# The MLP pairs of a four-layer vision transformer: transpositions moved into the second product, normalised rows first on VectorE

## What is computed

```python
for i in range(DEPTH):                         # DEPTH = 4
    ...                                        # attention: h = h + proj(attn(layernorm(h)))
    y = layernorm(h, ln2_w[i], ln2_b[i])
    y = gelu(y @ fc1_w[i] + fc1_b[i])          # 128 -> 256
    h = h + (y @ fc2_w[i] + fc2_b[i])          # 256 -> 128
```

## Time and profile before

| | |
|---|---|
| median of 3 runs | 4076.8 us (4069.07 to 4085.77) |
| the profiled execution: its time, its span | 4077.07 us, 4075.3 us |
| mean granted clock of PE | 0.945 of full speed |
| PE busy | 3523.8 us, 86% of the span |
| DVE, POOL, ACT busy | 2503.2, 2284.3, 1907.3 us |
| PE in 500 to 600 us (attention) | 96.54 us busy, 1129 matmuls |
| PE in 1400 to 1500 us (MLP of layer 1) | 85.25 us busy, 602 matmuls |
| PE in 2700 to 2800 us (mostly MLP of layer 3) | 85.41 us busy, 641 matmuls |

### The profile page before, as it was taken

The page is one execution under the profiler, slowest core; times in us unless marked ns, Lnnn a source line. Parts: engine busy times, 40 slices in busy tenths (PEclk is TensorE's granted clock), DMA queues, the critical chain, the costliest instruction groups (busy, mean ns, idle before and its releaser), DMA issues. The chain is left out here.

```text
span 4075.3 us, 91248 instructions
## 1 busy us (share of the span) xinstructions
PE 3523.8 (86%) x30780; PEld 2731.6 (67%) x30780; DVE 2503.2 (61%) x6419; ACT 1907.3 (47%) x3468; POOL 2284.3 (56%) x2633
## 2 busy tenths in 40 slices
PE   8779999888999888999987999988698887876983
PEld 8747777657777666777765777766344665655763
DVE  1246776546677555777654677755796887975110
ACT  0036666435666633666643666653464443322421
POOL 0056665465566366666446666625695663264876
PEclk9969999989999998999999999999898998998987
DMA  6556666025666314666502666620110223132432
GB/s 222 173 97 122 124 126 114 8 55 98 119 129 124 66 19 79 122 127 127 110 8 55 115 127 125 125 38 1 43 33 21 59 63 52 27 100 45 70 59 29
DMA packets 456050, 341.98 MB, mean 84 GB/s; under 512 B 70659, under 2 KB 440171, under 8 KB 455595
## 3 DMA queue, kind: packets, MB, share of 16 engines
q1 hardware_dynamic: 413635, 314.62, 37.5%
q0 software_dynamic: 27136, 16.42, 3.0%
q10 hardware_dynamic: 15008, 7.51, 0.7%
HBM read 227.69 MB, written 109.29 MB: 83 GB/s over the span
## 5 line engine op out<-in xcount | busy, mean ns | idle before, releaser
L720 DVE TENSOR_REDUCE a_neg_max<-a_S 99x4 f32<-99x788 f32 x1024 | 1003.5, 980 | 566.8 <-PE a_S L351 552.7
L533 ACT ACTIVATE a_probs<-a_St 99x792 f32<-99x792 f32 (+1 forms) x1024 | 851.2, 831 | 683.8 <-PE a_St L368 672.5
L368 PE MATMUL a_St<-a_q_st,a_k_st 99*99 99x198 bf16 (+1 forms) x4096 | 529.7, 252 | 90.5 <-DMA a_q_st<-a_max_rows 75.8
L351 PE MATMUL a_S<-a_k_st,a_q_st 96*99 96x197 bf16 x4096 | 552.1, 258 | 44.4 <-DVE a_neg_max L720 44.2
L351 PEld LDWEIGHTS a_S<-a_k_st,a_q_st 96*99 96x99 bf16 x4096 | 399.7, 128 | 266.5 <-DVE a_neg_max L720 220.4
L368 PEld LDWEIGHTS a_St<-a_q_st,a_k_st 99*99 99x99 bf16 (+1 forms) x4096 | 391.2, 126 | 122.5 <-DMA a_q_st<-a_max_rows 69.1
L385 PE MATMUL a_O<-a_probs,a_v_aug 99*32 99x198 f32 (+1 forms) x8192 | 466.4, 340 | 0.3
L663 POOL TENSOR_TENSOR h<-h,a_rows 99x512 f32<-99x512 f32 x128 | 162.8, 1272 | 275.1 <-DVE a_m_xn L801 275.1
L385 PEld LDWEIGHTS a_O<-a_probs,a_v_aug 99*32 99x32 f32 (+1 forms) x8192 | 247.0, 110 | 84.8 <-issue 2.1
L631 POOL CAST a_max_parts<-a_neg_max 99x32 bf16<-99x32 f32 x128 | 27.1, 212 | 471.1 <-DVE a_neg_max L720 471.1
L512 PEld LDWEIGHTS a_O<-a_w,a_gelu 128*99 128x99 f32 x2048 | 239.9, 167 | 45.0 <-issue 28.6
(11 more groups left out here) (263 smaller groups left out, 7314.2 us busy)
## 6 DMA issues: line engine op xcount, KB each, us to landing
xpatch<-in_x SPq DMA_DIRECT2D x64, 594.0 KB, 3.7
spill_q<-a_parts SPq DMA_DIRECT2D x384, 99.0 KB
spill_k<-a_parts SPq DMA_DIRECT2D x384, 99.0 KB
a_k_st<-spill_k SPq DMA_DIRECT2D x128, 297.0 KB, 4.2
a_q_st<-spill_q SPq DMA_DIRECT2D x128, 297.0 KB, 6.4
a_k_st<-spill_k SPq DMA_DIRECT2D x128, 198.0 KB, 4.7
a_q_st<-spill_q SPq DMA_DIRECT2D x128, 198.0 KB, 6.7
a_k_st<-spill_k SPq DMA_DIRECT2D x128, 99.0 KB, 5.0
```

What stands on the lines that cost most here:

```text
L351: mm = nc.tensor.matmul(S[0:TC, j // 2, j % 2 * TB:j % 2 * TB + NTOK], q_st[p % 4][0:SPLIT, head, b * TB + c * TC:b * TB + (c + 1) * TC], ...
L368: mm = nc.tensor.matmul(St[0:keys, j // 2, j % 2 * TB:(j % 2 + 1) * TB], k_st[p][:, head, first:first + keys], q_st[p][:, head, b * TB:(b ...
L533: nc.scalar.activation(probs[0:keys, u % 4, :].rearrange("p (x t) -> p x t", x=2), St[0:keys, :, 0:2 * TB], ACT.Exp).then_inc(s["probs"], 1)
L720: nc.vector.tensor_reduce(out.rearrange("p (x y) -> p x y", x=2), S[0:TC, :, 0:2 * TB].rearrange("p x (y t) -> p x y t", y=2)[:, :, :, 0:N ...
```

## The change

On PE, a helper `down(t)` issues the matmuls of one tile of L512. A call of `mlp` now issues L502 of pair k + 1, tile 0 of pair k, the waits and the four transpositions of pair k + 2, then tiles 1 to 3 of pair k, the last of which signals `m_fc2`. On DVE, L801 of pair k + 2 goes ahead of L795 and L809 of pair k + 3. The order on POOL and ACT isn't touched.

```diff
--- before.py
+++ after.py
@@ -492,6 +492,13 @@
 
                 def mlp(l, k, done):
                     m = layer_w[l]
+
+                    def down(t):
+                        for h in range(2):
+                            mm = nc.tensor.matmul(O[0:TC, t * D:(t + 1) * D], gl[k % 2][:, h, t * TC:(t + 1) * TC],
+                                                  m.w2[:, h * D:(h + 1) * D], start=(h == 0), stop=(h == 1))
+                        return mm
+
                     if 0 <= k + 1 < PAIRS:
                         n = at(l, k + 1)
                         if k == -1:
@@ -507,20 +514,20 @@
                             wait(pe, s["o_copied"], 2 * at(l, PAIRS))
                         wait(pe, s["m_gelu"], 2 * (n + 1))
                         wait(pe, s["m_h"], n)
-                        for t in range(4):
-                            for h in range(2):
-                                mm = nc.tensor.matmul(O[0:TC, t * D:(t + 1) * D], gl[n % 2][:, h, t * TC:(t + 1) * TC],
-                                                      m.w2[:, h * D:(h + 1) * D], start=(h == 0), stop=(h == 1))
-                        mm.then_inc(s["m_fc2"], 1)
+                        down(0)
                     if 0 <= k + 2 < PAIRS:
-                        n = at(l, k + 2)
-                        wait(pe, s["m_xn"], n + 1)
-                        wait(pe, s["m_yT"], n)
+                        n2 = at(l, k + 2)
+                        wait(pe, s["m_xn"], n2 + 1)
+                        wait(pe, s["m_yT"], n2)
                         wait(pe, s["yT"], at(l + 1, done + 6))
                         wait(pe, s["max_copied"], at(l + 1, done + 2))
                         for t in range(4):
-                            mm = nc.tensor.transpose(M2[:, t * TC:(t + 1) * TC], m_xn[n % 2][:, t, :], g.ident[0:TC, 0:TC])
+                            mm = nc.tensor.transpose(M2[:, t * TC:(t + 1) * TC], m_xn[n2 % 2][:, t, :], g.ident[0:TC, 0:TC])
                         mm.then_inc(s["m_turned"], 1)
+                    if 0 <= k < PAIRS:
+                        for t in range(1, 3):
+                            down(t)
+                        down(3).then_inc(s["m_fc2"], 1)
 
                 program(prep, attn, mlp)(pe)
 
@@ -786,6 +793,12 @@
                         row_max(l, i + 2, p + 2, 4)
 
                 def mlp(l, k, done):
+                    if 0 <= k + 2 < PAIRS:
+                        n = at(l, k + 2)
+                        wait(dve, s["m_rstd"], n + 1)
+                        wait(dve, s["m_turned"], n - 1)
+                        nc.vector.tensor_tensor(m_xn[n % 2][:], g.h[0:TC, (k + 2) * 4:(k + 3) * 4, :],
+                                                m_rstd[n % 2][:].to_broadcast([TC, 4, D]), ALU.mult).then_inc(s["m_xn"], 1)
                     if 0 <= k + 3 < PAIRS:
                         n = at(l, k + 3)
                         q = n % 2
@@ -794,12 +807,6 @@
                         for t in range(4):
                             op = nc.vector.bn_stats(m_stats[q][:, t, :], g.h[0:TC, (k + 3) * 4 + t, :])
                         op.then_inc(s["m_stats"], 1)
-                    if 0 <= k + 2 < PAIRS:
-                        n = at(l, k + 2)
-                        wait(dve, s["m_rstd"], n + 1)
-                        wait(dve, s["m_turned"], n - 1)
-                        nc.vector.tensor_tensor(m_xn[n % 2][:], g.h[0:TC, (k + 2) * 4:(k + 3) * 4, :],
-                                                m_rstd[n % 2][:].to_broadcast([TC, 4, D]), ALU.mult).then_inc(s["m_xn"], 1)
                     if 0 <= k + 3 < PAIRS:
                         n = at(l, k + 3)
                         q = n % 2
```

## The result

The changed kernel takes 4027.43 us (median of four runs, 4020.78 to 4032.26) where the kernel before took 4076.88 beside it (four runs, 4069.07 to 4085.77): a ratio of 0.9885, with 95% between 0.986 and 0.991. The forecast was 4016, its range 4001 to 4038. The profiled execution took 4020.78, 56.3 less than that of before.

What follows compares the result with a forecast made beforehand. PE, idle in each MLP pair for ACT's copy, was taken to bound the kernel. Gains of 3 x 13.3 + 24.0 = 63.9 us, less 2.4 for overlap, made 61.5: 4077.07 to 4016 us, range 4001 to 4038.

Steps and rivals of the forecast that it cites:

- Ordinary pair: MLP pair without preparation or attention steps: 4.28 us falls to 3.48, gaining 0.80, with ACT's copy covered by matmuls.
- POOL's ring: Loop through POOL and DVE from one xn (L801) to the next: 3.31 us, under PE's 3.48 by 0.17.
- Rivals 1, 3 and 4: In ordinary pairs: POOL loop at 3.8 us, 4043, chance 0.11; gain only 0.15, 4072, 0.04; slower, 4108, 0.03.
- rival 4: PE waits for late xn ahead of twelve matmuls that h needs: pair 4.54 us, total 4108, chance 0.03.
- Layer 3: Last layer's MLP stage, without attention blocks or preparation: 30 intervals at 0.80, a gain of 24.0 us.
- Preparation and pair 9: Layers 0 to 2: weight preparation on PE comes whole, 2.35 us, -2.0 a layer; xn late behind pair 9, -1.0.
- +0.38 for two intervals: Behind pairs 13 and 25, layers 0 to 2, where PE waits for POOL's xn: 0.38 us gained over two intervals.
- +0.38 for three: Behind pairs 17 and 21, layers 0 to 2, where POOL first makes bf16 parts: 0.38 us gained over three intervals.
- nothing gained: Behind pair 29, layers 0 to 2, scores and row maxima alternate between PE and DVE: no gain up to E(30).
- Rival 2: Longer PE standstill ahead of L451 brings the 1.2 GHz clock in 15 blocks: 16 us back, 4032, chance 0.07.
- A denser PE speaks against it: Argument against the clock falling to 1.2 GHz behind the longer standstill at L451; that case had chance 0.07.
- The overlap: In attention blocks, DVE's xn (L801) and POOL's L624 meet: 0.2 us each, 12 times, 2.4 us, from 0 to 8.

Runs made afterwards that it cites:

- e1: Changed kernel's PE order with DVE's order as in the kernel before (stats ahead of xn): 4101.37 us, ratio 1.0015 to the kernel before.
- e5: Changed kernel with DVE's old order behind pairs 13 to 29 and twelve unread matmuls in PE's standstill there, layers 0 to 2: 3998.64 us, ratio 0.98.
- e3: Changed kernel, but behind pairs 13, 17, 21, 25 and 29 DVE does xn after stats, so POOL's L631 runs first: 4032.75 us, ratio 0.9835.
- e4: Changed kernel with eight unread matmuls on PE behind pairs 13 to 29 in layers 0 to 2: 4019.63 us, ratio 0.98.
- e11: Kernel before, old orders, with eight unread matmuls behind pairs 13 to 25 and three behind scores: 4074.95 us, ratio 0.9958.
- e9: Changed kernel with DVE's old order in blocks, POOL's attention deviation earlier, two tiles ahead of the transpositions, and unread matmuls behind pairs and scores: 4005.87 us, ratio 0.9782.
- e2: Kernel before with only DVE's order changed, xn ahead of stats: 4087.52 us, ratio 0.9972 to the kernel before.

## Why the prediction was right, and where not

The side and the range were right, and so was the mechanism; 4016 was 11 us low by the medians, 5 us by the profiled executions (56.3 of 61.5). That it came so near is in part luck: layers 0 and 1 gained 8.2 and 3.5 us more than layer 2, because before had lost more there to its clock, and no term of the forecast had that. By its own steps:

- **Ordinary pair.** Forecast 3.48, measured 3.42. The four transpositions take their slot of 0.34 (2074.67 - 2074.32 = 0.35), not 0.40. 0.06 x 87 = 5 us more gain. No wait is left on PE; xn's slack and POOL's ring (3.31, measured 3.33) hold as worked out. Rivals 1, 3 and 4 did not come. e1 is rival 4's loop with its condition made true: 4.02.
- **Layer 3.** Forecast 24.0, measured 25.95: 24.75 from 29 ordinary intervals and 1.20 from the one without transpositions (4.28 to 3.08).
- **Preparation and pair 9.** Forecast 2.35 over the ordinary pair, measured 16.20 - 4 x 3.42 = 2.52, 0.17 more. Pair 9: forecast 1.0, measured 4.42 - 3.42 = 1.00.
- **The blocks: the step that failed.** "+0.38 for two intervals", "+0.38 for three" and "nothing gained" behind 29. In layer 2, with the ordinary intervals that belong to each, E(12) to E(14) is 11.56 + 3.42 = 14.98 (forecast 11.92); block 17 12.84 + 6.84 = 19.68 (18.80); 21 15.09 + 6.84 = 21.93 (18.81); 25 17.39 + 3.42 = 20.81 (22.20); 29 19.62 (17.28). Together 8.0 us lost. 13.3 + 0.4 (the first transpositions, which lie ahead of the first h) + 1.1 for 19 ordinary pairs - 0.2 - 8.0 = 6.6; measured 6.5. The sums for 13, 17 and 21 were right for a clock that stays (e5: 11.88, 18.80, 18.80). What the forecast put at nothing there was the clock behind a longer standstill. The 22.20 for 25 was taken from rows of before at the low clock; e5 has 18.05.
- **What took its place.** Rival 2, which the forecast priced as if it came wholly or not at all: 16 us at 0.07. It came in part. The standstill was worked out as 2.9 and is 2.95 without the collision (e3), 3.45 with it. Behind 13 the clock now fell in every layer, where before it had fallen in two of three; over the twelve blocks 13 to 25 the first product took more than 1.49 in nine before and in twelve after. It fell at different points: behind 13 at the end of the standstill, behind 17 and 25 only among the products that follow L451 (0.56), behind 29 among the scores. "A denser PE speaks against it" was the wrong argument: density on average did not keep the clock through the standstill. Filling it gives 12.9 (e4) and 24.0 us (e5 against e3). What the change itself lost to the clock is less than these, since before had lost at least 25 us too (e11). An estimate: e11 gave back 25.4 us for some 100 us at the lower level, e5 against e3 24.0 for some 105 (mean clock of layers 0 to 2 0.87 each in e3, 0.96, 0.99 and 0.97 in e5), so a us there cost 0.23 to 0.25, and the 40 us more of after cost 9 to 10, more than half of rival 2's 16.
- **The overlap.** Priced at 0.2 each, "since POOL is just first". DVE was first by 0.02, and POOL held for 0.50. That came behind 13, 17 and 21, nine times, 4.5 us in place of 2.4; behind 25 there was no meeting, and PE stood 2.95. But e3 removes it and gains nothing on balance, so the term had no net price while the clock was low. The Trainium skill (SBUF — State Buffer, section "Who interferes with whom") calls the port that two such instructions share an exclusive lock. The trace agrees on who waits, and nearly on how long (if the second waited for the whole first, L631 would take 1.04 + 0.64 = 1.68): L631 took 1.54 when xn was 0.02 ahead, 1.04 when it was not; in e9 xn took 1.46 (usually 0.68) when the bias L665 was 0.36 ahead. Of the two sums that I weighed by it, 63.9 and 55.9, none is borne out by this: the delay was there and cost nothing.
- **Layers 0 and 1.** The forecast gave all three layers the same 12.5. They gained 14.7 and 10.0, because their blocks before were longer than layer 2's (11.02 and 9.71 behind 13, where layer 2 had 8.02); after the change all three take 167.8 to 168.4. In block 13 of before, L502 took 2.85, 2.84 and 1.49 in layers 0, 1 and 2, behind the same standstill of 2.52. The prediction quotes the 1.49 of layer 2; rows of all three would have given the clock a higher chance.
- **Behind 29.** Forecast 17.28, measured 19.6 in every layer. The interval goes with the clock: 17.3 at a mean of 0.80 (before), 19.5 to 19.7 at 0.65 (e1, e2, after), 16.9 and 16.8 at 1.00 (e11 and e9, which fill among the scores). e1 and e2 each have it alone, e2 with ordinary pairs at 4.28, so it is not the denser ordinary pair that brings it.

Not settled: by what the clock stays low behind 29 for twice as long as before with either half of the change, and why it fell in some blocks and not in others of the same standstill.

## What to carry to other kernels

An order on PE that hides a hop needs its operand that much earlier: here neither half of the change was worth 0.5% (0.1 and 12.2 us of stages), and both together gave 57. After a change that makes the ordinary case denser, look at what the denser engine now waits for: the standstill can grow (here from 2.52 to 2.95 and 3.45), and its price may lie less in its length than in the clock behind it. Compare the same block in every layer before taking its rows for typical, and try a few matmuls that nobody reads where PE must stand still.

## What the runs showed of the hardware that I had not expected

- Behind a standstill of 1.75 us at L451 the first product took its 1.49 in eight blocks of nine (e2); behind 2.52 in three of twelve (before); behind 2.95 (e3) and 2.95 to 3.45 (after) in none of twelve each. Elsewhere it took 2.0 to 2.85. The length alone doesn't decide it: the ninth block of e2 had 2.85 behind 1.75.
- Eight filler matmuls (1.95 us) in the standstill behind pair 13 moved the fall from L451 to L509; twelve (2.84), with xn late, prevented it there. Ahead of the scores behind pair 29 they made the interval longer by up to 2.1, and in one layer of e5 shorter by 1.6, where the clock stayed at 1.00.
- xn on DVE, begun 0.02 us ahead of L631 on POOL, made that take 0.50 us longer, and the bias on POOL, begun 0.36 ahead of xn, made xn take 0.78 longer (e9: 1.46 for 0.68).
- The part of the program outside the stages, some 3400 us, took 3401.1 to 3441.2 in thirteen profiled executions: a change of 10 us can't be read from one total, though it can from its own stretch.
